# Two key tiles per value visit in a two-layer cross-attention kernel, with new order and piece tables

## What is computed

```python
# layer 0
K, V = heads(norm(ctx) @ Wk.T), heads(norm(ctx) @ Wv.T); Q = heads(x @ Wq.T)
x = x + tanh(gate) * (softmax(Q @ K.T * 0.25, mask) @ V) @ Wo.T
# layer 1
q = heads(norm(x) @ q_w + q_b); k, v = heads(ctx @ k_w + k_b), heads(ctx @ v_w + v_b)
h = x + (softmax(q @ k.T * 0.25, mask) @ v) @ cproj_w + cproj_b
out = h + gelu(norm(h) @ fc_w + fc_b) @ proj_w + proj_b
```

## Time and profile before

| | |
|---|---|
| median of 3 runs | 2141.55 us |
| profiled execution | 2143.75 us, span 2142.0 us, mean PE clock 0.953 of full |
| PE busy | 2015.5 us (94%) |
| DVE, ACT, POOL busy | 1419.6 (66%), 1262.7 (59%), 422.9 us (20%) |

### The profile page before, as it was taken

The page is one execution under the profiler, slowest core; times in us unless marked ns, Lnnn a source line. Parts: engine busy times, 40 slices in busy tenths (PEclk is TensorE's granted clock), DMA queues, the critical chain, the costliest instruction groups (busy, mean ns, idle before and its releaser), DMA issues.

```text
span 2142.0 us, 45507 instructions
## 1 busy us (share of the span) xinstructions
PE 2015.5 (94%) x14940; PEld 1067.4 (50%) x14940; DVE 1419.6 (66%) x2389; ACT 1262.7 (59%) x2327; POOL 422.9 (20%) x441
## 2 busy tenths in 40 slices
PE   6799999999999999999999999999999999999997
PEld 4344545454544545445455455545554454554544
DVE  3576777767666775767657676676766667676752
ACT  2165656567555674656646575566655557565673
POOL 2040113103231032311222022310213103111020
PEclk9799999999999999999999999999999999999998
DMA  5425151432414242151421515134151432315100
GB/s 149 121 73 143 49 145 35 108 87 82 91 42 114 75 126 54 51 143 36 132 62 47 126 50 137 47 86 109 43 130 42 100 87 89 84 51 113 29 2 10
DMA packets 139706, 176.80 MB, mean 83 GB/s; under 512 B 32020, under 2 KB 110013, under 8 KB 137397
## 3 DMA queue, kind: packets, MB, share of 16 engines
q1 hardware_dynamic: 137301, 170.65, 31.5%
q10 hardware_dynamic: 2144, 2.90, 0.5%
HBM read 125.33 MB, written 48.16 MB: 81 GB/s over the span
## 4 chain that ended last, share of the span: by engine, by line
PE 46%; issue 23%; POOL 11%; DMA 8%; SPq 7%; DVE 3%; ACT 2%; POOLq 0%; ACTq 0%; DVEq 0%
PE p_sc L1112 11%; PE p_acc L1145 11%; PE p_mx L1132 9%; PE p_misc L1180 7%; POOL ctxn L589 5%; DMA qst<-scr_q 4%; POOL parts L620 3%; SPq L489 3%; DMA scr_k<-parts 3%; SPq L502 2%; PE p_misc L1218 2%; PE p_misc L1206 2%; DVE maxes L867 1%; PE p_misc L1173 1%; PE p_misc L1166 1%
## 5 line engine op out<-in xcount | busy, mean ns | idle before, releaser
L867 DVE TENSOR_REDUCE maxes<-p_mx 128x1 f32<-128x802 f32 x1024 | 986.0, 984 | 404.5 <-PE p_mx L1132 401.8
L777 ACT ACTIVATE prob<-p_sc 128x512 f32<-128x512 f32 (+1 forms) x1664 | 926.3, 595 | 431.6 <-PE p_sc L1112 422.4
L1112 PE MATMUL p_sc<-qst,kst 100*128 100x256 bf16 (+1 forms) x3328 | 666.8, 283 | 23.6 <-ACT prob L777 11.6
L1132 PE MATMUL p_mx<-kst,qst 97*128 97x401 bf16 x2048 | 545.7, 349 | 52.6 <-DMA qst<-scr_q 44.3
L1145 PE MATMUL p_acc<-prob,vals 128*17 128x256 f32 x6656 | 538.5, 397 | 3.5 <-ACT o_raw L785 3.2
L1112 PEld LDWEIGHTS p_sc<-qst,kst 100*128 100x128 bf16 (+1 forms) x3328 | 267.8, 101 | 530.0 <-ACT prob L777 224.7
L620 POOL TENSOR_TENSOR parts<-rest,parts 128x512 bf16<-128x512 f32 (+1 forms) x144 | 139.5, 969 | 696.2 <-DVE parts L958 696.1
L1132 PEld LDWEIGHTS p_mx<-kst,qst 97*128 97x128 bf16 x2048 | 195.1, 100 | 105.4 <-DMA qst<-scr_q 28.3
L1145 PEld LDWEIGHTS p_acc<-prob,vals 128*17 128x17 f32 x6656 | 111.3, 96 | 253.3 <-issue 195.1
L1180 PE MATMUL p_misc<-wv,ctxt 128*128 128x256 f32 x800 | 197.4, 389 | 2.0 <-DVE rest L947 2.0
L1173 PE MATMUL p_misc<-ctxt,wk 128*128 128x512 f32 x488 | 191.5, 515 | 1.0 <-ACT vals L731 0.7
(11 more groups left out here) (143 smaller groups left out, 1083.5 us busy)
## 6 DMA issues: line engine op xcount, KB each, us to landing
kst<-scr_k SPq DMA_DIRECT2D x96, 400.2 KB
kst<-scr_k SPq DMA_DIRECT2D x192, 200.1 KB
scr_k<-parts SPq DMA_DIRECT2D x96, 384.0 KB, 3.2
ctxn<-in_ctx_dram SPq DMA_DIRECT2D x16, 1536.0 KB
scr_q<-parts SPq DMA_DIRECT2D x16, 384.0 KB, 2.9
qst<-scr_q SPq DMA_DIRECT2D x96, 64.0 KB, 9.3
qst<-scr_q SPq DMA_DIRECT2D x192, 32.0 KB, 2.5
xin<-in_x_dram SPq DMA_DIRECT2D x8, 256.0 KB, 2.8
```

Of the source, the lines that this page charges most:

```text
L777: act.activation(prob[0:rows, u % 2, 2 * half:2 * half + 2, :].rearrange("p h t -> p (h t)"), p_sc[0:rows, half, :], ACT.Exp).then_inc(exp ...
L867: dve.tensor_reduce(maxes[:, c:c + 1], p_mx[:, c % 2, :, 0:CW], AX.XY, ALU.max).then_inc(chunk_done, 1)
L1112: ins = mm(p_sc[0:rows, half, T * q:T * q + T], kst[0:RB, h, P * j:P * j + rows], qst[0:RB, h, :], start=True, stop=True)
L1132: ins = mm(p_mx[:, c % 2, w, 0:CW], qst[0:RA, h, P * t:P * t + P], kst[0:RA, h, s0:s0 + CW], start=True, stop=True)
```

## The change

A value visit takes two tiles, those of units u - 1 and u - 2 (tile 0 of a group alone), so a group has 7 visits (6 double) instead of 13. Visits stand in units with u % 13 in {0, 1, 3, 5, 7, 9, 11}. `prob` has three slots instead of two, and the waits count visits. The order in a unit is now both score halves, MX, visit, chunk, piece, second chunk. The chunk table is the same in all groups, 2 chunks in the units without a visit. The 16th chunk of a group is now the first chunk of u % 13 = 8; before, it stood in u = 7, 20, 34 and 46. Normalizing the context of even loop blocks moves from POOL to DVE. Both layers have one table of prep pieces. `bias_row` lies in `z`.

```diff
-DOUBLES = ({6, 7, 12, 15, 17, 23, 28, 33, 39, 41, 45, 51},
-           {5, 7, 12, 14, 19, 23, 25, 30, 37, 40, 44, 49})
+CHUNKS_AT = (1, 1, 2, 0, 2, 1, 2, 0, 2, 0, 2, 1, 2)
-PREP0_AT = {3: T0, 6: T1, 8: T2, 10: T3, 11: T4, 12: K00, 14: T5, 15: K01, 16: T6, 17: K02, 18: XT, 20: K03,
-  23: Q, 25: K10, 27: K11, 31: V0, 33: K12, 36: K13, 38: V1, 40: V2, 43: V3, 45: V4, 49: V5, 51: V6}
-PREP1_AT = {1: T0, 2: T1, 3: T2, 4: T3, 6: T4, 8: T5, 11: T6, 14: K00, 16: K01, 18: K02, 19: XT, 20: K03,
-  23: Q, 25: K10, 28: K11, 30: K12, 33: K13, 36: V0, 38: V1, 40: V2, 43: V3, 45: V4, 49: V5, 51: V6}
+PREP0_AT = PREP1_AT = {1: T0, 2: T1, 3: T2, 4: T3, 6: T4, 8: T5, 10: T6, 12: K00, 15: K01, 17: K02, 19: K03,
+  21: XT, 23: Q, 25: K10, 28: K11, 30: K12, 32: K13, 34: V0, 36: V1, 38: V2, 41: V3, 43: V4, 45: V5, 49: V6}
-POST1_AT = {5: WO0, 7: WO1, 10: HT, 12: FC0, 17: FC1, 27: FC2, 32: FC3, 37: PJ0, 41: PJ1}
-APPLY_AT = {0: 0, 1: 1, 4: 2, 5: 3, 7: 4, 8: 5, 11: 6}
+POST1_AT = {5: WO0, 7: WO1, 11: HT, 13: FC0, 20: FC1, 27: FC2, 33: FC3, 40: PJ0, 42: PJ1}
+APPLY_AT = {0: 0, 1: 1, 2: 2, 3: 3, 4: 4, 6: 5, 8: 6}
+def slot(u):
+    return (u - 2 * min(max(u - 1, 0), 2 * NT)) % SLOTS
 # weigh
-                for q in range(HG):
-                    ins = mm(p_acc[...], vals[...], prob[0:rows, u % 2, q, :], ...)
+                for v in (u - 1, u) if u % NT else (u,):
+                    j = v % NT
+                    for q in range(HG):
+                        ins = mm(p_acc[...], vals[...], prob[0:rows, slot(v), q, :], ...)
 # visit on PE
                         scores(blk, u, 0)
+                        scores(blk, u, 1)
                         if piece and piece[0] == "MX":
                             do_piece(blk, piece)
-                        if cs:
-                            chunk(blk, *cs[0])
-                        scores(blk, u, 1)
-                        if len(cs) > 1:
-                            chunk(blk, *cs[1])
-                        if piece and piece[0] != "MX":
-                            do_piece(blk, piece)
+                        if u % NT == 1:
+                            chunk(blk, *cs.pop(0)) if cs else None
                         if u == 0:
                             if blk.n0 > 0:
                                 weigh_last_of_before(blk)
-                        else:
+                        elif ends_visit(u - 1):
                             weigh(...)
+                        if cs:
+                            chunk(blk, *cs[0])
+                        if piece and piece[0] != "MX":
+                            do_piece(blk, piece)
+                        if len(cs) > 1:
+                            chunk(blk, *cs[1])
```

More of the change, by code:

```diff
@@ L202, in unit_chunks @@
         return []
-    doubles = DOUBLES[blk.prep == 1]
-    first = 16 + EARLY + u + sum(d < u for d in doubles)
-    every = range(first, first + 1 + (u in doubles))
+    first = 16 + EARLY + 16 * (u // NT) + sum(CHUNKS_AT[:u % NT])
+    every = range(first, first + CHUNKS_AT[u % NT])
     return [(c // 16, c % 16) for c in every if blk.n0 < 15 or c // 16 < NG]
@@ L210, in tile_pair, with slot_before, ends_visit, visits_through @@
     return range(2 * k, min(2 * k + 2, NT))
+def slot(u):
+    return (u - 2 * min(max(u - 1, 0), 2 * NT)) % SLOTS
+def slot_before(u):
+    earlier = [v - UNITS for v in range(UNITS)] + list(range(u))
+    return next(v for v in reversed(earlier) if slot(v % UNITS) == slot(u))
+def ends_visit(u):
+    return u % NT % 2 == 0
+def visits_through(u):
+    return VISITS * (u // NT) + (u % NT + 1) // 2 + 1
 def product_rows(j):
@@ L774, in exps @@
                     act.wait_ge(scores_ready, k + 1)
-                    if half == 0 and (blk.n0 > 0 or u >= 2):
-                        act.wait_ge(weighed, UNITS * blk.n + u - 1)
-                    act.activation(prob[0:rows, u % 2, 2 * half:2 * half + 2, :].rearrange("p h t -> p (h t)"),
+                    if half == 0 and (blk.n0 > 0 or slot_before(u) >= 0):
+                        act.wait_ge(weighed, NG * VISITS * blk.n + visits_through(slot_before(u)))
+                    act.activation(prob[0:rows, slot(u), 2 * half:2 * half + 2, :].rearrange("p h t -> p (h t)"),
                                    p_sc[0:rows, half, :], ACT.Exp).then_inc(exp_done, 1)
@@ L992, in visit @@
                     fold_first()
-                    ctx_apply(dve, blk, range(NT))
+                    ctx_apply(dve, blk.prep_b, range(NT))
                 if blk.n0 == 16:
@@ L1136, in weigh @@
             def weigh(par, units_before, G, u, first):
-                g, j = u // NT, u % NT
-                rows = tile_rows(j)
+                g = u // NT
                 pe.wait_ge(exp_done, 2 * units_before + 2)
-                if j == 0 and not first:
+                if u % NT == 0 and not first:
                     pe.wait_ge(acc_saved, G)
-                for q in range(HG):
-                    h = HG * g + q
-                    ins = mm(p_acc[32 * q:32 * q + VW, 0:T],
-                             vals[par][0:rows, j, h, :], prob[0:rows, u % 2, q, :],
-                             start=(j == 0), stop=(j == NT - 1))
+                for v in (u - 1, u) if u % NT else (u,):
+                    j = v % NT
+                    rows = tile_rows(j)
+                    for q in range(HG):
+                        h = HG * g + q
+                        ins = mm(p_acc[32 * q:32 * q + VW, 0:T],
+                                 vals[par][0:rows, j, h, :], prob[0:rows, slot(v), q, :],
+                                 start=(j == 0), stop=(j == NT - 1))
                 ins.then_inc(weighed, 1)
```

34 lines of the change are left out of this document (17 added, 17 removed), and 9 rows, old and new, of tables (PREP0_AT, PREP1_AT).

## The result

| | before | after |
|---|---|---|
| median of 4 runs each | 2143.42 us | 2209.26 us (2207.2 to 2212.41) |
| ratio to before | | 1.0302, 95% interval 1.0273 to 1.0331 |
| span of the profiled execution | 2142.0 us | 2210.6 us |
| mean PE clock | 0.953 | 0.946 |
| PE busy | 2015.5 us | 1953.4 us |

What follows compares the result with a forecast made beforehand. PE, busy 94% of the span, was taken as the bound. 2143.75 - 77 - 6 + 64 + 63 + 5 + 8 + 23 = 2223.75, some 2.2 above the median; forecast 2220 us, likeliest case 2190 to 2255, wider range 2142 to 2262.

Steps and rivals of the forecast that it cites:

- double visits: Value visits on PE: merging two tiles saves a 0.20 us strip passage 384 times, -77 us, bounds 0 to -92.
- MX before a visit: MX right before a visit, both in narrow strips, saves about 0.1 us 63 times: -6 us, bounds 0 and -12.
- maximum wait: PE waits before MX for DVE's split of the maxima, with too little work after chunk 16: +64 us, bounds 0 and +85.
- u = 34: ACT waits at K(1, 3)'s save for K(1, 1)'s store behind the key fetch, stalling PE: +63 us, bounds -20 and +80.
- clock: PE at half speed after longer MX waits and the lengthened u = 34 wait: +23 us, bounds -15 and +60.
- Exps: Second score half needs the previous unit's second Exp, so short units wait on ACT: +5 us, bounds 0 and +20.
- normalizing on DVE: Context normalization on DVE, u = 0 to 8 of 6 blocks, delays T3 at u = 4: +8 us, bounds 0 and +17.
- the stagger of 0.02: Within a visit, about 0.02 us added to two passes of 0.216, making 0.45 us per tile.
- exposed weights: Rival in double visits: second tile's weight loads not hidden, about 0.09 us per added tile, +35, total 2255; chance 0.10.
- not paid: Rival at MX: splits end sooner or PE comes later, -64 and -15 of the clock, total 2141; chance 0.08.
- buffer free in time: Rival at u = 34: K(1, 1)'s store lands early, +63 and some 8 of clock go, total 2149; chance 0.10.

Runs made afterwards that it cites:

- experiment 4: Experiment 2's and experiment 1's edits together, each double visit split, one tile between the score halves, the other at the visit's old place; 2115.71 us, 0.985 to the kernel before.
- experiment 7: The kernel before with only double visits and three probability slots, keeping its old order, tables and normalization on POOL; 2120.97 us, 0.9875 to the kernel before.
- Experiment 2: The changed kernel with MX moved behind the value visit of its unit on PE; 2171.44 us, 1.0107 to the kernel before.
- experiment 3: The changed kernel with K(1, 3) at u = 36, V0 and V1 at 32 and 34, and MX behind the visit; 2063.74 us, 0.96 to the kernel before.
- experiment 1: The changed kernel with K(1, 3) moved from u = 32 to 36, V0 and V1 to 32 and 34; 2114.14 us, 0.9853 to the kernel before.
- 11: The same kernel as experiment 3, run again on another chip; 2065.67 us, 0.9632 to the kernel before.
- experiment 5: Experiment 1 with a group's 16th chunk moved from u % 13 = 8 to second of 6, one chunk from 12 to 5; 2119.29 us, 0.9869 to the kernel before.
- 10: Experiment 3 with first fetch at u = 25, V0, V1, K(1, 2) at 30, 32, 34, and V6 moved from u = 49 to 51; 2063.52 us, 0.9617.
- 12: Experiment 3 with V6 moved from u = 49 to 51; 2056.16 us, 0.9597 to the kernel before.
- experiment 6: The changed kernel with the query fetch issued at u = 28 instead of 26, behind the store of K(1, 1); 2170.8 us, 1.011 to the kernel before.

## Why the prediction was right, and where it was not

| step | predicted | measured |
|---|---|---|
| double visits | -77 | 384 x 0.22 = -84 |
| MX before a visit | -6 | 63 x 0.17 = -11 |
| maximum wait | +64 | +56 |
| u = 34 | +63 | +47 |
| GELU step at u = 32, odd blocks | not foreseen | +8 |
| clock | +23 | -2 |
| Exps | +5 | about +14 |
| normalizing on DVE | +8 | not apart |
| loop's back edge | not foreseen | +11 |
| other short gaps of PE | not foreseen | about +20 |
| not found | | about +10 |
| span | 2142.0 + 80 = 2222 | 2210.6 |

**The visits.** Right, and a little low: the added tile costs 0.432, its two passes alone; the stagger of 0.02 that I charged is not paid twice. That rules out the exposed weights: they would have made it 0.54. The rule against which I weighed this (the Trainium skill, "TensorE: Matmul & The Clock Gate", Part 3, as I put it) would keep a load on the same rows from overlapping; here all sixteen loads use the same rows, and the measurement decides for the trace. The same Part also lets a load into the background weight buffer overlap, which I left out; no run shows which buffer these loads go to. That a narrow strip costs an entry and an exit agrees with the Trainium skill, "TensorEngine Tiling (Array Packing)", Key Properties, "Mode switching requires drain"; the price is this case's 0.22 us. The merging saved less time than it saved PE's work: experiment 4 got 52 of the 84 and experiment 7 only 27.

**MX before a visit.** Right, and too low. From MX to the visit behind it pass 10 to 121 ns, 83 in the mean (120 or 121 in half of the 63, as 599.37 to 599.49 in the rows above), and the visit's own entry of 0.09 us falls away; before, 168 ns passed in the mean from MX to the chunk behind it. That is 0.17 us saved each time.

**The maximum wait.** Right in its mechanism and nearly in size. From the last score ahead of MX to MX pass 1.147 us in the mean over 63, where 0.202 would do: 59.5 us, against 3.1 before. Six of these waits, 7.7 us, are for the bank p_misc and not for the split, which the prediction did not have. (Before, the third group's 16th chunk stood in u = 33, not 34.) Experiment 2 took 42 of it back and experiment 3 shows 47 to 54 beside an otherwise quiet kernel; the rival "not paid" is out.

**u = 34.** Right for the even blocks: with block 1 seven waits of 8.2 to 8.5 us and one of 6.9 (8.2 predicted). The odd ones wait 2.9 to 4.6 us at FC3 where I had 6.2. Two things that I did not have bring PE there later. It has stopped for 1.26 us at the scores of u = 32 (815.79 above), which comes from a GELU step and not from the buffer: experiment 1 has it too. And in four of the six odd blocks the clock had fallen before PE reached FC3; there the wait is 2.9 to 3.9 us, in the other two 4.5 and 4.6. So 65.5 us at the scores and 21.8 at FC3 stand against 35.1 less for the queries and 5.0 that the scores of u = 35 waited before: 47, and 7.5 apart for u = 32. Experiment 1 removed the waits at u = 34 by moving one piece, by 96 us, the slow stretches behind them included; the rival "buffer free in time" is out, since this store landed 8.5 to 10.4 us after its issue (median of the 96 stores of its size over the kernel: 3.4).

**The clock.** This step failed. The stretches around the wait of block 4 (us, busy us of PE, PEld, DVE, ACT, POOL, then PEclk, DMA share, GB/s):

```profile
687.00:695.50 8.50, 0.03 (x4) 0.00 (x0) 0.39 (x2) 0.78 (x3) 0.00 (x0) 0.74 0.85 182
695.50:700.00 4.50, 4.42 (x13) 3.21 (x14) 1.93 (x7) 1.60 (x4) 0.31 (x1) 0.50 0.08 11
700.00:701.30 1.30, 1.30 (x5) 0.57 (x5) 0.00 (x0) 0.51 (x1) 0.00 (x0) 0.51 0.00 0
701.30:705.00 3.70, 3.70 (x35) 2.61 (x34) 2.10 (x3) 2.26 (x5) 0.00 (x0) 1.00 0.01 3
```

PE did nothing for 8.5 us, for about half of which the clock had already fallen (0.74 in the mean), and then ran 5.7 us at the lower level (1.2 GHz); over the eight such waits it was 3.2 to 5.8 us. Over the kernel the time at that level grew from 202 to 240 us, but only time in which PE works there costs anything, and that went from 177.8 to 173.9 us: -2, not +23. By place, before and after, in us of PE's work at the lower level:

| | before | after |
|---|---|---|
| first 200 us | 33.5 | 40.1 |
| around u = 34 | 90.2 | 74.1 |
| at the loop's back edge | 37.6 | 39.0 |
| at MX, behind the first 200 us | 0 | 6.8 |
| last 75 us | 16.4 | 13.9 |

The waits at u = 34 were followed by a slow stretch before as well; they got longer, not more, and the slow work behind them shrank. Of the waits at MX, for which I had charged 20, only three of the eight longest (1.6 to 2.0 us) were followed by one, with 13 us of work in all, so some 7 us lost. Experiment 2, which takes these waits away, still has 174.1 us, but 50.7 of them in the first 200 us, so its total does not settle this. The mean granted clock of a kernel, 0.946 against 0.953, misleads here, since it counts the waits. Where the waits at u = 34 go (experiment 1), the slow working time falls to 105.2 us, 34 gained. These are single executions, and two of one kernel differ by up to 19 us of such work (experiments 3 and 11).

**Not foreseen.** The GELU step at u = 32, above. And the edge of the loop, from 2.1 to 2.3 us before to between 4.0 and 4.9 us, five times. No engine is waited for. Two edits shorten it: one chunk instead of two at the end of the loop's body (from experiment 1 to experiment 5: 4.8 to 3.0 us in the mean) and MX behind the visit (from the change to experiment 2: 4.4 to 3.5); V6 at the end gives little (3.3, experiments 10 and 12). What sets its length stays open.

**Short gaps.** The visits, MX, the waits, the clock and the edge come to 2142.0 - 84 - 11 + 56 + 47 + 8 - 2 + 11 = 2167, 44 below the span. Most of that lies in gaps that the list of waits hardly shows. PE has 138 gaps before and 300 after (111.4 and 241.0 us), and each also lays bare the modelled tail of the matmul ahead of it, 0.16 us. Among those under 0.5 us: ahead of a second score half, 66 under 0.2 us, 4.9 us in all, where there were 6 (0.4); with the tails 66 x 0.16 + 4.9 = 15, 14 more than before. That is the step on the Exps, whose upper bound was 20. Ahead of a piece, behind a chunk: 48, 8.7 us, with tails 16, among them the 7.7 us in which key pieces wait for DVE's bank. Ahead of a chunk, behind a piece: 27, 1.4 us, with tails 6. What normalizing on DVE adds to the second of these I did not take apart. Other classes shrank or grew by less. Over all gaps the rise is 129.6 us and 162 tails of 0.16, 156 in all; 122 of it is named above (56 + 47 + 8 + 11), which leaves 34 for all short gaps and some 10 us that I did not find. So I was right on the total partly by luck: 25 too much for the clock, 24 too much for the two large waits and 12 too little for what visits and MX save, against 63 (8 + 11 + 44) where I had 13 for all the rest.

## What to carry to other kernels

Where several narrow matmuls can go side by side, put as many as dependencies allow behind one entry; but count what the removed PE time was covering, because a good part of it can come back as waits (84 us of work gone were worth 52 in one order and 27 in another, where the clock gave part of the 27). Before a piece is moved, ask which buffer it needs, whose transfer frees that buffer, and what stands behind the waiting instruction on its engine: here the place of one piece was worth more than the 384 merged visits. The wait for an engine in arrears was not cured here by feeding that engine earlier (experiment 5), but by putting other work of the waiting engine in front (experiment 2). And before the clock is named as a cause, compare two executions of one kernel: here, on two chips, they differed by 12 us, 9 of them the clock's.

## What the runs showed of the hardware that was not expected

- An added tile in a narrow strip costs its passes alone, 0.432 us = 2 x 0.216; entering and leaving the strip costs 0.22 once. From a 17-column visit to a 24-column matmul no exit is paid (0.875 us from start to start in experiment 2, where other work comes at 0.99); the other way round 10 to 121 ns pass.
- A store of 384 KB right behind 13 bulk transfers on one queue lands 8.5 to 10.4 us after its issue; 92 of the kernel's 128 key stores land in under 5 us, 2.8 in the median. This also when only half of them stand ahead of it (experiment 6: 8.5 to 11.1 in the loop). The Trainium skill, "DMA: Bandwidth & Descriptors", "Queues, rings and completion order", has the descriptors of one queue taken up in order on each DMA engine, while a later one may finish before an earlier one; no run here shows which of the later ones delayed the store.
- Waits of 1.0 to 1.5 us at MX left the clock alone in the loop, those of 8 us at u = 34 were followed by 3.2 to 5.8 us at 1.2 GHz. Short waits were not always harmless: before, two waits of 0.9 to 1.7 and 0.3 to 1.4 us some 2 us apart (queries, then Exps, at u = 34 of odd blocks) were followed by a slow stretch in all six.
- A loop edge on PE costs 2.0 to 5.1 us in kernels that differ only in the work around it, and 6.7 to 9.2 us at 1.2 GHz follow each one after the change.
